# Two attentions of a fused transformer block: who copies and normalises the turned output, who scales the rows of maxima, and in which blocks the loads are issued

## The chip, the cores and the metric

The kernel runs on one core of one Trainium2 chip. The metric is the time of one execution in microseconds of the device, the median of three runs. A core has a matrix engine (TensorE, PE in the profile, with PEld for its weight loads), VectorE (DVE), ScalarE (ACT), GpSimd (POOL) and SyncE (SP), each with its own instruction queue; they meet in semaphores. DMAs are issued by POOL on queue q0 and by SP on queue q1, and are worked off by 16 DMA engines.

## The reference

```
x = x + L0(groupnorm(x))            # attention with relative positions, 12 heads of 16, 1024 tokens per image
t = tokens(x)
t = t + L1_attn(layernorm(t))       # attention without them
t = t + L1_ffn(layernorm(t))        # 16 experts, each token goes to one

L0:      attn = q*scale @ k^T + rel_h[..., :, None] + rel_w[..., None, :]
         out  = softmax(attn) @ v ;  return out @ proj_w + proj_b
L1_attn: softmax(q @ k^T / sqrt(192)) @ v
```

The batch is 8 images of 1024 tokens with 192 channels. The change is in `attention`, which computes the scores, the softmax and the product with v of both attentions.

## The kernel before

The stages follow one another: projections of the first attention (p1), the first attention (a1, with relative positions), output projection and projections of the second (p2), the second attention (a2), routing and experts. `attention` is called twice, with `rel` true and false.

One attention is 24 **steps**, one for each image and group of 4 heads. Steps come in pairs (u = 0, 1) with two sets of buffers; the first and the last pair are written out, the ten between them are a loop on each engine. A step has 16 **blocks**: 2 halves of the queries (512 each) times 8 tiles of 128 keys. In a block PE computes the 4 heads' scores, keys on partitions, into psS (L371); ACT takes the exponential into a_probs, two heads at a time (L458); PE multiplies by the values of the block before (L382, "pv"), which sums the turned output, 4 heads of 32 rows by 512 queries, in psO over the 8 key tiles. The value tile's 17th column is one, so that the row sums come along.

Exponentials need each query's row maximum beforehand. So PE also computes, one to two steps ahead, scores with queries on partitions from other buffers (a_qmax, a_kmax and, for even steps, h_qmax, h_kmax), 64 "max" jobs a step, 4 in a block (L353), and DVE reduces each to its maximum (L503). After the last of them, in block 12, DVE joins the two halves of the keys (L508). In block 13 a "rows" job turns the 128 by 32 maxima on PE (L357), DVE scales them to f16 (L513), and SP stores them as an extra row of a_qrows (L266), so that the score matmul subtracts them. From block 13 on (MAXBLK) the max jobs belong to the step after next; their buffers' loads are waited for at the start of that block (loadedm).

When a half is done, ACT copies the turned output out of psO (L449), a "back" job, four transposes on PE (L361), turns it back, DVE takes the reciprocal of the row sums (L520) and multiplies (L523), and SP stores the result (L280). Back jobs run at the end of blocks 2 (for the half before) and 10.

Max, rows and back jobs share psR, a ring of three PSUM banks: job n may start when job n-3 has been read. All readers of the ring are on DVE:

```
elif j[0] == "rows":                 # L513
    nc.vector.tensor_scalar(MT[:, :], psR[0:UNITS, slot, 0:P], -1.0 / MAXSCALE, None, ALU.mult)
else:                                # L520, L523
    nc.vector.reciprocal(RC[:, :, :], o[:, :, HD:HD + 1])
    nc.vector.tensor_tensor(OS[:, qh, :, :], o[:, :, 0:HD], RC..., ALU.mult)
```

The order on PE in a block is: scores of both pairs, two max jobs, pv of the block before, (rows in block 13,) two max jobs, (back in blocks 2 and 10).

Loads for later steps are issued by POOL, block by block. POOL's entry for block k waits until pv of block k-1 is done, which PE runs in the middle of its block k. `load_maxima` (L214) loads a_qmax and a_kmax, or the h_ ones, for the step after next: in a1 in entries 0 to 4, in a2 in entries 0 to 7, one query and one key part in each. `load` (L225) loads a_qrows, a_krows and a_v for the next step: the terms of queries and keys in a1 in entries 5, 6, 7 (three of 128 KB in each), rows for relative widths and heights in entries 8 to 11 (256 KB and 64 KB); in a2 the terms in entries 8 to 11; values in 12 and 13. In a1 SP also writes, two blocks ahead, 8 rows for relative heights into a_qrows before each block with kt >= 2 (`rel_rows`, L274, a_qrows<-relh, 32 KB); PE waits for them (relrow) at the start of that block.

Of the kernel before, what the change touches and what calls it, by code (L numbers as in the profile page):

```python
# [13 lines left out]
P = 128  # L14
# [4 lines left out]
GH = 4  # L19
# [23 lines left out]
def attention(nc, name, rel, scale, QK, RL, RLH, VN, OD, onehot_dram, head, early=None):  # L43
# [13 lines left out]
    with ExitStack() as ctx:  # L57
# [19 lines left out]
        OT = sb("outT", [P, QH, 512], F32)  # L77
        RC = sb("recip", [P, 4 * GH, 1], F32)
# [16 lines left out]
        ring_free = sem("ring_free")  # L95
        maxed = sem("maxed")
# [11 lines left out]
        SCORES, PVS, HALFS = 2 * BLK, BLK, QH  # L108

        def jobs_of(u, first, last):  # L110
            after = [[] for _ in range(BLK + 1)]
            for blk in range(BLK):
                offset, j = (1, EARLY + PER_BLK * blk) if blk < MAXBLK else (2, PER_BLK * (blk - MAXBLK))
                if not (last and u + offset >= 2):
                    after[blk] += [("max", j + i, offset) for i in range(PER_BLK)]
# [7 lines left out]
            return after  # L123

        FIRST = [("max", j, 0) for j in range(HALVES)] + [("rows",)] + [("max", j, 1) for j in range(EARLY)]
        PROLOGUE = len(FIRST)

        def number(first, last):
            at, out = 0, []
            for u in range(2):  # L130
                after = []
                for js in jobs_of(u, first, last):
                    after.append([(at + n, j) for n, j in enumerate(js)])
                    at += len(js)
                out.append(after)
            return out, at
# [4 lines left out]
        BASE0 = PROLOGUE  # L141
        BASE1 = PROLOGUE + N_FIRST

        def base_of(i):
            return BASE1 + (i - 1) * N_BODY
# [4 lines left out]
        def slot_free(n):  # L150
            return n + 2 if n < 2 else n + 1

        assert N_BODY % 3 == 2
        SHIFT = (1 - (BASE1 - 1)) % 3

# [3 lines left out]
        def back_number(jobs, u, which, qh):  # L159
            return next(n for js in jobs[u] for n, j in js if j[0] == "back" and j[1] == which and j[2] == qh)  # L160

        def rows_number(jobs, u):
            return next(n for n, j in jobs[u][MAXBLK] if j[0] == "rows")

        def max_of(j):
            r, half, p, qt = j % 2, j // 2 % 2, j // 4 % 2, j // 8
            return r, half, p, qt, r * 16 + p * 8 + qt
# [13 lines left out]
        def _(pool):  # L181
            def load_terms(s, buf, n):
                at = slice(HD * n, HD * n + HD)
                for c in range(NA):
                    pool.dma_start(A[buf][c][at, :, :], qk(s, TERMS[n][0], 0)).then_inc(loaded[buf], 16)  # L185
                pool.dma_start(K[buf][at, :, :], qk(s, TERMS[n][1], 1)).then_inc(loaded[buf], 16)

            def load_rel(s, buf, c, half):
                w, h = QR + WI * half, RH + 4 * half
                pool.dma_start(A[buf][c][w:w + WI, :, :], rel_w(s, half)).then_inc(loaded[buf], 16)  # L190
                if half == 0:
                    pool.dma_start(A[buf][c][RH:RH + 8, :, :], RLH[s, c].rearrange("i (k h) t -> (i k) h t", h=GH))\
                        .then_inc(loaded[buf], 16)
# [5 lines left out]
            def load_max_terms(s, buf, r, n):  # L199
                of = slice(64 * r + HD * n, 64 * r + HD * n + HD)  # L200
                pool.dma_start(AM[buf][0][of, :, :], qk_pair(s, TERMS[n][0], 0, r)).then_inc(loadedm[buf], 16)  # L201
                pool.dma_start(KM[buf][of, :, :], qk_pair(s, TERMS[n][1], 1, r)).then_inc(loadedm[buf], 16)

            def load_max_rel(s, buf, r, half):
                am, at = AM[buf][half], 64 * r
                if half == 1:
                    pool.dma_start(am[at:at + HD, :, :], qk_pair(s, 0, 0, r)).then_inc(loadedm[buf], 16)
                pool.dma_start(am[at + HD:at + HD + WI, :, :],
                               RL[s, 0].rearrange("(k r p) t -> r k p t", p=2, r=2)[r]).then_inc(loadedm[buf], 16)
                pool.dma_start(am[at + HD + WI:at + 64, :, :],  # L210
# [3 lines left out]
            def load_maxima(s, buf, blk):  # L214

                if rel:
                    if blk == 0:
                        load_max_terms(s, buf, 0, 0)
                        load_max_terms(s, buf, 1, 0)
                    elif blk < 5:  # L220
                        load_max_rel(s, buf, blk % 2, (blk - 1) // 2)
                elif blk < 8:
                    load_max_terms(s, buf, blk % 2, blk // 2)

            def load(s, buf, blk):  # L225

                if rel:
                    if blk in (5, 6, 7):
                        load_terms(s, buf, blk - 5)
                    elif blk in (8, 9, 10, 11):  # L230
                        load_rel(s, buf, blk % 2, (blk - 8) // 2)
                elif blk in (8, 9, 10, 11):
                    load_terms(s, buf, blk - 8)
                if blk in (12, 13):
                    load_values(s, buf, blk - 12)

# [3 lines left out]
            for blk in range(BLK):  # L240
# [4 lines left out]
            pool.wait_ge(ring_free, HALVES + 4)  # L245

            def step(s, u, last):
                for blk in range(BLK):
                    pool.wait_ge(pvdone, s * PVS + blk + 2)
                    nc.gpsimd.sem_inc(paced, 1)  # L250
                    if not last:
                        load_maxima(s + 2, u, blk)
                    load(s + 1, 1 - u, blk)

            with pool.Fori(0, ITERS - 1) as i:
                for u in range(2):
                    step(2 * i + u, u, False)
            step(STEPS - 2, 0, True)

        @block.sync  # L260
        def _(sp):
            def row_of_maxima(buf, free):

                sp.wait_ge(ring_free, free)
# [12 lines left out]
            def store(s, qh, base, n):  # L277

                sp.wait_ge(ring_free, base + n + 4)
# [27 lines left out]
            row_of_maxima(0, HALVES + 4)  # L307

            def step(i, u, jobs, base, first, last):
# [4 lines left out]
                for blk in range(BLK):  # L314
# [11 lines left out]
                    if blk == 4 and not (first and u == 0):  # L326
                        store(s - 1, 1, base, back_number(jobs, u, -1, 1))
                    if blk == KT + 4:
                        store(s, 0, base, back_number(jobs, u, 0, 0))
                if more:  # L330
                    row_of_maxima(1 - u, base + rows_number(jobs, u) + 4)
                else:
                    store(s, 1, base, back_number(jobs, u, 0, 1))
# [12 lines left out]
        def _(pe):  # L346
            def job(jn, j, base, slot, free, buf, halves, rows):
                pe.wait_ge(ring_free, base + free)
                if j[0] == "max":
                    r, half, p, qt, _ = max_of(j[1])  # L350
                    b = (buf + j[2]) % 2
                    at = slice(64 * r, 64 * r + MR)
                    mm = nc.tensor.matmul(psR[:, slot, :], AM[b][half][at, p, P * qt:P * qt + P],  # L353
                                          KM[b][at, p, 512 * half:512 * half + 512], start=True, stop=True)
# [10 lines left out]
            def scores_pair(buf, kt, qh, pair, n, pairs):  # L365

                pe.wait_ge(exped, pairs + n + 1)
                for j in range(2):
                    keys, queries = slice(P * kt, P * kt + P), slice(512 * qh, 512 * qh + 512)
# [16 lines left out]
            def step(i, u, jobs, base, first, last, slot, free):  # L386
# [1432 lines left out]
```

## Time and profile before

| what | value |
|---|---|
| median of 3 runs | 3230.5 us (3227.85 to 3234.65) |
| span of the profiled execution, first to last instruction | 3278.2 us, 47.7 us over that median; no time around it is given |
| busy: PE, DVE, ACT, POOL | 2922.2, 2439.8, 1849.7, 1061.6 us |
| mean granted TensorE clock | 0.906 |

The span is read by stages: scores of a1 start between 365 and 1457 us, those of a2 between 1796 and 2841 us. Within an attention the timeline (instructions in order of time, merged where they follow one another) repeats with the block. A row of the timeline gives the start, the length, the engine, the line of the kernel, the operation, output<-input, the number of instructions, and in brackets the engine's idle time before it and what ended it. "SPq" and "POOL ... DMA" rows are issues of DMAs, not transfers.

### The profile page before, as it was taken

To read this page: it belongs to the slowest core of one execution; us is meant where nothing else is said; L and a number is where in the kernel's file an instruction comes from. 1 tells how busy PE (TensorE), PEld (TensorE's weight loads), DVE (VectorE), ACT (ScalarE), POOL (GpSimd) and SP (SyncE) were. 2 spreads that over 40 slices of the span, in tenths; PEclk is the share of its full clock that TensorE was granted. 3 is DMA by queue.
4 is the path that set the end of the run, shared out by engine and by line. 5 is a ranking of instruction groups with operands and counts; after the bars stand their busy time and mean duration, and the time that the engine had idled before them with its cause. 6 is when DMAs were issued, how large, how long until landed. Compare 5 with 4: busy or idle time off the path is not lost. (4 is left out here: it accounts for less than half of the span.)

```text
span 3278.2 us, 63755 instructions
## 1 busy us (share of the span) xinstructions
PE 2922.2 (89%) x17818; PEld 1147.0 (35%) x17818; DVE 2439.8 (74%) x4430; ACT 1849.7 (56%) x2379; POOL 1061.6 (32%) x1714
## 2 busy tenths in 40 slices
PE   5886999999999999977897999999999999871887
PEld 4664122222222222215652222222222222361666
DVE  4544899999999999933547999999999999451221
ACT  2433376667776677663440677777777777610332
POOL 0012233333333333213232333232333332155665
PEclk9776799999999999998995999999999999965777
DMA  6776554555445554433654622222222222350211
GB/s 126 219 237 184 104 103 98 100 110 107 102 101 100 111 103 100 90 61 121 206 160 98 124 72 70 72 75 75 73 76 75 70 71 63 97 89 12 58 54 35
DMA packets 222364, 327.92 MB, mean 100 GB/s; under 512 B 63820, under 2 KB 150550, under 8 KB 217650
## 3 DMA queue, kind: packets, MB, share of 16 engines
q0 software_dynamic: 79488, 202.00, 27.3%
q1 hardware_dynamic: 142772, 124.60, 14.5%
q8 instruction: 56, 0.92, 0.1%
q14 instruction: 48, 0.39, 0.1%
HBM read 217.71 MB, written 109.19 MB: 100 GB/s over the span
## 5 line engine op out<-in xcount | busy, mean ns | idle before, releaser
L458 ACT ACTIVATE a_probs<-a_psS 128x1024 f32<-128x1024 f32 x1536 | 1488.5, 1021 | 738.5 <-PE a_psS L371 734.0
L503 DVE TENSOR_REDUCE h_halfmax<-a_psR 128x1 f32<-128x512 f32 x1536 | 979.7, 686 | 73.5 <-PE a_psR L353 64.3
L503 DVE TENSOR_REDUCE a_halfmax<-a_psR 128x1 f32<-128x512 f32 x1536 | 984.2, 686 | 63.6 <-PE a_psR L353 54.5
L371 PE MATMUL a_psS<-a_qrows,a_krows 121*128 121x512 f16 (+1 forms) x3072 | 804.2, 383 | 44.8 <-DMA a_qrows<-relh 40.2
L382 PE MATMUL a_psO<-a_probs,a_v 128*32 128x512 f32 x6144 | 824.0, 609 | 1.2 <-ACT a_probs L458 1.2
L353 PE MATMUL a_psR<-h_kmax,h_qmax 64*128 64x512 f16 x1536 | 357.9, 405 | 40.8 <-POOL h_ident L39 40.1
L371 PEld LDWEIGHTS a_psS<-a_qrows,a_krows 121*128 121x128 f16 (+1 forms) x3072 | 241.8, 98 | 417.7 <-issue 161.5
L353 PE MATMUL a_psR<-a_kmax,a_qmax 64*128 64x512 f16 x1536 | 325.6, 393 | 1.8 <-DVE a_halfmax L503 1.4
L353 PEld LDWEIGHTS a_psR<-h_kmax,h_qmax 64*128 64x128 f16 x1536 | 81.9, 93 | 539.1 <-DVE h_halfmax L503 471.6
L353 PEld LDWEIGHTS a_psR<-a_kmax,a_qmax 64*128 64x128 f16 x1536 | 78.9, 93 | 490.4 <-DVE a_halfmax L503 460.1
L185 POOL DMA_DIRECT2D a_qrows<-qk x240 | 124.1, 517 | 264.5 <-PE a_psO L382 262.0
L861 PE MATMUL p_psQ<-p_xnT,p_wqk 96*128 96x512 f32 x384 | 183.0, 640 | 16.0 <-DVE p_xnT L1015 13.9
L382 PEld LDWEIGHTS a_psO<-a_probs,a_v 128*32 128x32 f32 x6144 | 121.2, 108 | 183.3 <-issue 176.3
L201 POOL DMA_DIRECT2D h_qmax<-qk x110 | 56.3, 512 | 358.4 <-PE a_psO L382 305.2
L1628 DVE TENSOR_TENSOR e_y<-e_psY,e_x 128x192 f32<-128x192 f32 x80 | 28.6, 357 | 191.1 <-PE e_psY L1553 106.6
L201 POOL DMA_DIRECT2D a_qmax<-qk x120 | 61.4, 512 | 301.3 <-PE a_psO L382 300.5
L1049 DVE SCALAR_TENSOR_TENSOR p_half<-p_qk,p_sc,p_half 128x2048 f16<-128x2048 f32 (+1 forms) x36 | 71.5, 1997 | 103.1 <-ACT p_half L958 103.1
L951 ACT ACTIVATE p_qk<-p_psQ,p_bqk 128x512 f32<-128x512 f32 x96 | 65.9, 686 | 114.6 <-PE p_psQ L861 114.6
L1590 ACT COPY e_xmT<-e_psX 96x256 f32<-96x256 f32 x80 | 29.5, 369 | 175.0 <-PE e_psX L1547 130.5
L861 PEld LDWEIGHTS p_psQ<-p_xnT,p_wqk 96*128 96x128 f32 x384 | 77.5, 206 | 117.1 <-issue 107.3
L190 POOL DMA_DIRECT2D a_qrows<-rel x96 | 48.6, 506 | 205.6 <-PE a_psO L382 205.6
L197 POOL DMA_DIRECT2D a_v<-v x96 | 53.8, 560 | 185.4 <-PE a_psO L382 184.7
(185 smaller groups left out, 2755.2 us busy)
## 6 DMA issues: line engine op xcount, KB each, us to landing
a_qrows<-qk POOLq DMA_DIRECT2D x240, 128.0 KB, 4.2
qk<-p_half SPq DMA_DIRECT2D x96, 256.0 KB, 3.3
a_qrows<-rel POOLq DMA_DIRECT2D x96, 256.0 KB, 4.2
a_v<-v POOLq DMA_DIRECT2D x96, 256.0 KB, 3.1
a_krows<-qk POOLq DMA_DIRECT2D x168, 128.0 KB, 4.5
v<-p_v SPq DMA_DIRECT2D x36, 512.0 KB, 5.7
relh<-p_rel SPq DMA_DIRECT2D x48, 256.0 KB
attn<-a_out SPq DMA_DIRECT2D x96, 128.0 KB, 2.3
```

The costliest lines, as they stand in the source:

```text
L185: pool.dma_start(A[buf][c][at, :, :], qk(s, TERMS[n][0], 0)).then_inc(loaded[buf], 16)
L190: pool.dma_start(A[buf][c][w:w + WI, :, :], rel_w(s, half)).then_inc(loaded[buf], 16)
L197: pool.dma_start(V[buf][:, x, :, :], VN[s][:, x, :, :]).then_inc(loaded[buf], 16)
L201: pool.dma_start(AM[buf][0][of, :, :], qk_pair(s, TERMS[n][0], 0, r)).then_inc(loadedm[buf], 16)
L353: mm = nc.tensor.matmul(psR[:, slot, :], AM[b][half][at, p, P * qt:P * qt + P], KM[b][at, p, 512 * half:512 * half + 512], start=True, sto ...
L371: mm = nc.tensor.matmul(psS[:, (2 * n + j) % 4, :], K[buf][:, h, keys], A[buf][kt % NA][:, h, queries], start=True, stop=True)
L382: mm = nc.tensor.matmul(psO[32 * h:32 * h + 32, :], V[buf][:, kt, h, :], PT[:, blk % 2, h, :], start=(kt == 0), stop=(kt == KT - 1))
L458: nc.scalar.activation(PT[:, blk % 2, 2 * pair:2 * pair + 2, :], psS[:, b0:b0 + 2, :], ACT.Exp, scale=scale).then_inc(exped, 1)
L503: nc.vector.tensor_reduce(mx[:, unit, half:half + 1], psR[:, slot, :], AX.X, ALU.max)\
L861: mm = nc.tensor.matmul(psQ[:, n % 2, :], WQK[:, c, P * m:P * m + P], XN[:, c, 512 * q:512 * q + 512], start=(c == 0), stop=(c == 1))
L951: nc.scalar.activation(QF[:, m, 512 * q:512 * q + 512], psQ[:, n % 2, :], ACT.Identity, bias=BQK[:, m:m + 1], scale=1.0).then_inc(qf, 1)
L1049: half = nc.vector.scalar_tensor_tensor(HL[1][:, m, tokens], QF[:, m, tokens], SC[:, m:m + 1], HL[0][:, m, tokens], ALU.mult, ALU.subtract)
```

## The change

The psR ring gets two more readers. ACT copies the turned output of a back job from psR to a new SBUF tile a_outTurned (semaphore copied); DVE takes the reciprocals from there; POOL multiplies, in its entries 4 and 12, ahead of that entry's loads (semaphore normed); SP's store waits for normed. ACT also scales the rows of maxima. ACT does both between the exponentials of two blocks, DVE the reciprocal a block later, after that block's first two reductions. Ring slots freed by ACT are counted apart from those that DVE frees. The rows job moves behind the last two max jobs of block 13; in the first 64 maxima before step 0 it moves behind two jobs of the next step.

```diff
-                after[MAXBLK].insert(2, ("rows",))
+                after[MAXBLK].append(("rows",))
...
+            def normalise(steps, qh):
+                pool.wait_ge(recips, steps * QH + qh + 1)
+                pool.wait_ge(stored[qh], steps * 16 + 16)
+                nc.gpsimd.tensor_tensor(OS[:, qh, :, :], OB[:, :, 0:HD], RC[:, :, :].to_broadcast([P, 4 * GH, HD]),
+                                        ALU.mult).then_inc(normed, 1)
...
+                if j[0] == "rows":
+                    nc.scalar.activation(MT[:, :], psR[0:UNITS, slot, 0:P], ACT.Copy, scale=-1.0 / MAXSCALE).then_inc(copied, 1)
+                else:
+                    half = s * QH + j[1] * QH + j[2]
+                    act.wait_ge(normed, half)
+                    nc.scalar.copy(OB[:, :, :].rearrange("p x v -> p (x v)"), psR[:, slot, :]).then_inc(copied, 1)
...
+            def reciprocals(at, base, s):
+                dve.wait_ge(copied, base[2] + at[2] + 1)
+                dve.wait_ge(normed, half)
+                nc.vector.reciprocal(RC[:, :, :], OB[:, :, HD:HD + 1]).then_inc(recips, 1)
```

The loads are the same ones, issued in other entries:

```diff
             def load_maxima(s, buf, blk):
+                if rel and 2 <= blk < 6:
+                    load_max_query(s, buf, blk % 2, (blk - 2) // 2, 0)
+                    load_max_height(s, buf, blk % 2, (blk - 2) // 2)
+                elif rel and blk in (6, 7):
+                    load_max_key(s, buf, blk % 2, 0)
+                elif rel and 8 <= blk < 12:
+                    load_max_width(s, buf, blk % 2, (blk - 8) // 2)
+                if not rel and blk < 8:
+                    load_max_query(s, buf, blk % 2, 0, blk // 2)
+                elif not rel and 8 <= blk < 12:
+                    load_max_key(s, buf, 0, blk - 8)
+                    load_max_key(s, buf, 1, blk - 8)
             def load(s, buf, blk):
                 if rel:
+                    if blk < 3:
+                        load_query(s, buf, 0, blk)
+                        load_query(s, buf, 1, blk)
+                    elif blk < 7:
+                        load_width(s, buf, blk % 2, (blk - 3) // 2)
+                    elif blk == 7:
+                        load_key(s, buf, 0)
+                        load_key(s, buf, 1)
+                    elif blk == 8:
+                        load_key(s, buf, 2)
+                        load_height(s, buf, 0)
+                        load_height(s, buf, 1)
                 elif blk < 8:
+                    (load_query(s, buf, 0, blk // 2) if blk % 2 == 0 else load_key(s, buf, blk // 2))
```

PE's waits for these loads (loaded at block 0, loadedm at block 13, relrow) stand where they stood.

First place: POOL in the loop of a1, first step of a pair, entries 6 to 9 (a1_qrows1, a1_krows1: the next step's buffers; h1_qmax0: those of the maxima two steps on). Before:

```order
L185 DMA a1_qrows1_0<-qk1 16x4x1024
L185 DMA a1_qrows1_1<-qk1 16x4x1024
L186 ISA
L186 DMA a1_krows1<-qk1 16x4x1024
L249 REGISTER_ALU
L190 DMA a1_qrows1_0<-rel1 32x4096
L192 DMA a1_qrows1_0<-relh1 8x4096
L249 REGISTER_ALU
L190 DMA a1_qrows1_1<-rel1 32x4096
L192 ISA
L192 DMA a1_qrows1_1<-relh1 8x4096
```

and now, entries 7 to 9:

```order
L224 DMA h1_kmax0<-qk1 16x2x1024
L204 ISA
L204 DMA a1_krows1<-qk1 16x4x1024
L204 ISA
L204 DMA a1_krows1<-qk1 16x4x1024
L291 REGISTER_ALU
L228 DMA h1_qmax0_0<-rel1 32x2048
L204 DMA a1_krows1<-qk1 16x4x1024
L211 DMA a1_qrows1_0<-relh1 8x4096
L211 ISA
L211 DMA a1_qrows1_1<-relh1 8x4096
```

The run of nine query and key loads followed by the width and height rows is gone; query terms and widths went to entries 0 to 6, and one width part for the maxima is now issued in each of entries 8 to 11.

Second place: POOL in the loop of a2, entries 10 to 13. Before:

```order
L185 DMA a2_qrows1<-qk2 16x4x1024
L186 DMA a2_krows1<-qk2 16x4x1024
L249 REGISTER_ALU
L197 ISA
L197 DMA a2_v1<-v2 128x512
```

and now:

```order
L224 DMA h2_kmax0<-qk2 16x2x1024 x2
L291 REGISTER_ALU
L224 DMA h2_kmax0<-qk2 16x2x1024 x2
L291 REGISTER_ALU
L274 ISA
L275 REGISTER_ALU
L276 TENSOR_TENSOR a2_out<-a2_outTurned,a2_recip 128x256
L216 ISA
L216 DMA a2_v1<-v2 128x512
```

The key parts for the maxima two steps on moved here, two in each of entries 8 to 11, and the multiplication stands ahead of the first values.

Third place: PE in the loop of a2, block 13 from its pv on (psR is the ring). Before:

```order
L382 MATMUL a_psO<-a_probs,a_v 32x512 x4
L348 REGISTER_ALU
L356 REGISTER_ALU
L357 MATMUL a_psR<-h_ident,h_rowmax 32x128
L348 REGISTER_ALU
L353 MATMUL a_psR<-h_kmax,h_qmax 128x512
```

and now:

```order
L435 MATMUL a_psO<-a_probs,a_v 32x512 x4
L401 REGISTER_ALU
L406 MATMUL a_psR<-h_kmax,h_qmax 128x512
L401 REGISTER_ALU
L406 MATMUL a_psR<-h_kmax,h_qmax 128x512
L401 REGISTER_ALU
L409 REGISTER_ALU
L410 MATMUL a_psR<-h_ident,h_rowmax 32x128
```

The turning of the maxima moved behind the pair of max jobs.

## Rows read from the trace of the kernel before

**Rows 1.** The page: its first row.
```profile
span 3278.2 us, 63755 instructions
```
**Rows 2.** Line L371 (scores): a1's stretch, then a2's; starts of first and last.
```profile
L371 PE MATMUL a_psS<-a_qrows,a_krows x1536: 377/379/634, 365.0 to 1456.5; 121*128 121x512 f16 x192
...
L371 PE MATMUL a_psS<-a_qrows,a_krows x1536: 377/379/634, 1796.4 to 2840.4; 65*128 65x512 f16 x192
```
**Rows 3.** Timeline of a2, one block: scores, two maxima, pv, next scores.
```profile
2162.76 1.04 PE L371 MATMUL a_psS<-a_qrows,a_krows 65*128 65x512 f16 x4
...
2163.74 0.39 PE L353 MATMUL a_psR<-a_kmax,a_qmax 64*128 64x512 f16 x2
...
2164.05 1.06 PE L382 MATMUL a_psO<-a_probs,a_v 128*32 128x512 f32 x8
...
2165.38 1.04 PE L371 MATMUL a_psS<-a_qrows,a_krows 65*128 65x512 f16 x4
```
**Rows 4.** Busy time by engine, 82 us inside a2: PE, PEld, DVE, ACT, POOL.
```profile
2132.00:2214.00 82.00, 81.63 (x498) 21.96 (x496) 79.35 (x132) 59.79 (x64) 25.57 (x50) 1.00 0.29 76
```
**Rows 5.** Timeline before step 0 of a2: DVE's 64 reductions, then scaling the rows.
```profile
1750.65 38.36 DVE L503 TENSOR_REDUCE h_halfmax<-a_psR 128x1 f32<-128x512 f32 x64 [15.70 <-PE a_psR L353]
...
1789.80 0.28 DVE L513 TENSOR_SCALAR h_rowmaxT<-a_psR 32x128 f16<-32x128 f32 x1 [0.56 <-PE a_psR L357]
```
**Rows 6.** What PE waited for in a1, 400 to 1440 us: total, times, longest.
```profile
PE a_psS L371 <- DMA a_qrows<-relh: 37.9, 22, 2.4
```
**Rows 7.** Timeline of a1, blocks 8 to 10: issue of rows, scores.
```profile
805.03 7.50 SPq L274 DMA_DIRECT2D a_qrows<-relh  x3
...
806.43 1.04 PE L371 MATMUL a_psS<-a_qrows,a_krows 121*128 121x512 f16 x4
...
810.66 1.03 PE L371 MATMUL a_psS<-a_qrows,a_krows 121*128 121x512 f16 x4 [1.55 <-DMA a_qrows<-relh]
```
**Rows 8.** DMA issues, 799 to 811 us: KB each, median us to landing.
```profile
a_qrows<-qk POOLq DMA_DIRECT2D x6, 128.0 KB, 4.5
```
**Rows 9.** DMA issues, 785 to 799 us, the same.
```profile
a_qmax<-rel POOLq DMA_DIRECT2D x4, 128.0 KB, 2.6
a_qmax<-qk POOLq DMA_DIRECT2D x4, 64.0 KB, 2.3
```
**Rows 10.** Timeline of a1: POOL's entry 11, then PE's scores of block 13.
```profile
817.22 0.49 POOL L190 DMA_DIRECT2D a_qrows<-rel  x1 [3.03 <-PE a_psO L382]
...
819.41 1.04 PE L371 MATMUL a_psS<-a_qrows,a_krows 121*128 121x512 f16 x4
```
**Rows 11.** Timeline of a2: POOL's entry 11, then PE's scores of block 13.
```profile
2184.71 0.51 POOL L185 DMA_DIRECT2D a_qrows<-qk  x1 [2.10 <-PE a_psO L382]
...
2185.25 0.51 POOL L186 DMA_DIRECT2D a_krows<-qk  x1
...
2186.86 1.04 PE L371 MATMUL a_psS<-a_qrows,a_krows 65*128 65x512 f16 x4
```
**Rows 12.** Timeline of a2, block 13 from pv to the next scores.
```profile
2188.15 1.06 PE L382 MATMUL a_psO<-a_probs,a_v 128*32 128x512 f32 x8
...
2189.15 0.28 PE L357 MATMUL a_psR<-h_ident,h_rowmax 128*32 128x128 f32 x1
...
2189.37 0.76 PE L353 MATMUL a_psR<-h_kmax,h_qmax 64*128 64x512 f16 x2
...
2190.06 1.04 PE L371 MATMUL a_psS<-a_qrows,a_krows 65*128 65x512 f16 x4
```
**Rows 13.** Timeline of a2 after a back job: ACT, DVE.
```profile
2160.88 1.94 ACT L458 ACTIVATE a_probs<-a_psS 128x1024 f32<-128x1024 f32 x2 [1.28 <-PE a_psS L371]
...
2161.35 0.43 DVE L523 TENSOR_TENSOR a_out<-a_psR,a_recip 128x256 f32<-128x256 f32 x1
```
**Rows 14.** Groups by line: ACT's copy of psO, and POOL's addition of a bias.
```profile
L449 ACT COPY a_outT<-a_psO 128x512 f32<-128x512 f32 x96 | 56.7, 591 | 5.5 <-PE a_psO L382 3.6
...
L791 POOL TENSOR_TENSOR p_x<-p_x,p_bproj 128x3072 f32<-128x3072 f32 x4 | 26.7, 6686 | 32.6 <-DMA p_x<-in_x 32.6
```

More of the change, by code:

```diff
@@ L107, in attention, with max_of @@
         NREL = 6
-        SCORES, PVS, HALFS = 2 * BLK, BLK, QH
+        SCORES, PVS = 2 * BLK, BLK
+        def max_of(j):
+            r, half, p, qt = j % 2, j // 2 % 2, j // 4 % 2, j // 8
+            return r, half, p, qt, r * 16 + p * 8 + qt
         def jobs_of(u, first, last):
-            after = [[] for _ in range(BLK + 1)]
+            before, after = [[] for _ in range(BLK + 1)], [[] for _ in range(BLK + 1)]
             for blk in range(BLK):
@@ L140, in attention, with other_number @@
         JOBS_LAST, _ = number(False, True)
-        BASE0 = PROLOGUE
-        BASE1 = PROLOGUE + N_FIRST
+        BASE1 = tuple(x + y for x, y in zip(BASE0, N_FIRST))
+        assert N_BODY[0] % 3 == 2
         def base_of(i):
-            return BASE1 + (i - 1) * N_BODY
+            return tuple(x + (i - 1) * y for x, y in zip(BASE1, N_BODY))
         def slot_of(n):
             return n % 3
[L150 to L154, printed above, removed]
+        SHIFT = (1 - (BASE1[0] - 1)) % 3
         def first_slot(m):
             return (m + SHIFT) % 3
[L159 to L167, printed above, removed]
+        def other_number(jobs, u, job):
+            return next(at[2] for a, b in jobs[u] for at in a + b if at[3] == job)
         block = ctx.enter_context(nc.Block())
@@ L403, in last_pv @@
[L403 to L407 removed]
                     scores_pair(u, kt, qh, 0, 2 * blk, 2 * blks)
                     scores_pair(u, kt, qh, 1, 2 * blk + 1, 2 * blks)
[L411 to L413 removed]
+                    for at in before:
+                        job(at, base, slot(at[0]), u, halves, s + 1)
@@ new lines, in step @@
+            def step(i, u, jobs, base, first, last, slot):
+                s = 2 * i + u
+                for blk in range(BLK):
+                    for at in jobs[u][blk - 1][1] if blk > 0 else []:
+                        if at[3][0] != "max":
+                            other(at, base, slot(at[0]), s)
+                    for pair in range(2):
+                        n = 2 * blk + pair
+                        act.wait_ge(scores, s * SCORES + n + 1)
+                        act.wait_ge(pvdone, s * PVS + blk + 1)
+                        b0 = 2 * n % 4
+                        nc.scalar.activation(PT[:, blk % 2, 2 * pair:2 * pair + 2, :], psS[:, b0:b0 + 2, :], ACT.Exp,
+                                             scale=scale).then_inc(exped, 1)
+                    if blk == 0 and not (first and u == 0):
+                        copy_out(s - 1, 1)
+                    if blk == KT:
+                        copy_out(s, 0)
+                if last and u == 1:
+                    copy_out(s, 1)
+                    for at in jobs[u][BLK][1]:
+                        other(at, base, slot(at[0]), s)
@@ L481, in _ @@
+            for at in FIRST:
+                if at[3][0] == "rows":
+                    other(at, (0, 0, 0), first_slot(at[0]), None)
             for u in range(2):
-                step(0, u, True, False, before_first)
-            step_1 = before_in(base_of(1), BASE0, JOBS_FIRST, JOBS)
+                step(0, u, JOBS_FIRST, BASE0, True, False, lambda n: first_slot(BASE0[0] + n))
+            with act.Fori(1, ITERS - 1) as i:
+                for u in range(2):
+                    step(i, u, JOBS, base_of(i), False, False, slot_of)
```

292 lines of the change are left out of this document (137 added, 155 removed).

## Prediction

> **What bounds the kernel now.** I read the span first [rows 1], then the two stages that the change touches. Both attentions issue the same 1536 score matmuls; from first to last a1 takes 1456.5 - 365.0 = 1091.5 us, a2 2840.4 - 1796.4 = 1044.0 us [rows 2]. So a1 loses 47.5 us that a2 doesn't.
>
> Then one block in the timeline. From scores to scores it takes 2165.38 - 2162.76 = 2.62 us, and the pieces touch: the maxima start 0.98 us after the scores, pv 0.31 us after them, the next scores 1.33 us after pv with two more maxima between [rows 3]. No piece waits: PE is busy for 81.63 of 82 us. DVE is busy for 79.35 of them and looks like a bound too [rows 4]. It isn't quite. Where nothing else paces DVE, before step 0, it does 64 reductions in 38.36 us, 0.60 each [rows 5]; four make 2.40 us, 0.2 us less than a block. PE sets the pace, DVE follows closely behind.
>
> Last, what stops PE in a1: the rows for relative heights, 22 times in the steady part, 37.9 us in all, up to 2.4 us at once [rows 6]. One case: SP issues the rows for block 10 at 805.03, block 9 starts at 806.43, and block 10 should start 2.62 us later, at 809.05, but starts at 810.66 [rows 7]. So the rows took some 5.5 us. In that stretch the 128 KB query loads, three per block with the key, take a median of 4.5 us [rows 8]; in the calmer stretch before it a 128 KB load takes 2.6 us and a 64 KB load 2.3 us [rows 9]. The rows are late because nine loads of 128 KB are issued ahead of them in three blocks, faster than they land.
>
> **The change part by part.** The sum is made against the profiled execution, whose span of 3278.2 us [rows 1] lies 47.7 us above the median of the runs; I take the differences over to the median unscaled.
>
> *Multiplication and row scaling leave DVE.* Per step that is 2 x 0.43 us [rows 13] and 0.28 us [rows 5], 1.14 us; the reciprocals stay. Worth nothing on the path, since PE paces the block; if DVE were the cover that is gone, see the first rival.
>
> *ACT's copies.* The copy of the turned output has the size of the copy out of psO, 0.59 us [rows 14]. It falls in the gap after a back job, where ACT sat idle for 1.28 us waiting for the next scores [rows 13]. What queues behind it, the next exponentials, then starts at most 0.1 us later, and pv needs these only a block later. Row scaling is smaller and falls in the same kind of gap. Cost: zero, at most 3 x 0.1 us a step.
>
> *POOL's multiplication.* 3072 elements per partition took 6.69 us [rows 14], 2.2 ns each, so 256 take 0.56 us; with a start-up of as much again 1.1 us. Before that entry's loads: entry 12's values are needed in the next step, three blocks later. Cost zero. SP's store now waits for it, and the height rows of blocks 7 and 15 queue behind the store; they have two blocks, so I take zero here too and count any lateness in the fourth term.
>
> *The loads* are the same in number, and carry the sum.
>
> 1. The nine loads no longer pile up ahead of the heights: -47.5 us. The waits counted directly give 37.9 [rows 6], the lower bound; I take the difference of the stages, since their other work is equal.
>
> 2. In a1 one width part of 128 KB now leaves in entry 11, and PE waits for it before the scores of block 13, not only before the maxima. Entry 11 issues at 817.22, block 13 starts at 819.41: 2.19 us [rows 10]. At 2.6 us for landing [rows 9] PE stands for 0.41 us in each of the 22 steps that load maxima: +9.0 us. Bounds: 0, and 4.5 - 2.19 = 2.3 us a step if it lands as in the crowded stretch [rows 8]. I take the calm row, since entries 9 to 11 issue one load each.
>
> 3. In a2 entry 11 issues two key parts, the second 0.54 us after the first, as the two loads there do now, with 2186.86 - 2184.71 = 2.15 us to block 13 [rows 11]. A 64 KB load takes 2.3 us [rows 9]: 0.54 + 2.3 - 2.15 = 0.69 us, 22 times: +15.2 us. Bounds: 0.5 and, crowded, 2.9 us a step. The Trainium skill (DMA: Bandwidth & Descriptors, Anatomy of one DMA) gives a DMA a fixed 2.0 us and its bytes at 436 GB/s; by it, as an estimate, the key would land after 2.15 us and the sum would be 3 us less, but it would also have the 128 KB loads land in 2.3 us, where the trace shows 4.5.
>
> 4. Height rows that are still late: entries 2 to 5, 7 and 8 issue three or four loads. Between 0 and 0.9 us a step; block 12, behind entry 8's key and two height parts, is the likeliest. I take 0.4 us: +8.8 us.
>
> 5. The turning of the maxima. Today pv to the next scores takes 1.91 us in block 13 [rows 12] against 1.33 in another block [rows 3], 0.58 more: 0.22 us for the transposition, the rest because the last maxima no longer run as a pair. Behind the pair, the transposition costs between 0.22 and 0.58 us. And a PE that stood at the start of block 13 finds DVE further ahead. I take a gain of 0.2 us in the 44 steps that wait: -8.8 us.
>
> 6. The ends. The two early maxima ahead of the turning cover DVE's wait and scaling of 0.56 + 0.28 us [rows 5] before each step 0; the last half of each attention passes through ACT, DVE and POOL, about 1 us longer than now. Zero, bounds -2 and +2 us.
>
> Sum: -47.5 + 9.0 + 15.2 + 8.8 - 8.8 = -23.3 us. The span would be 3254.9, the median **3207 us**.
>
> **The rivals.**
>
> *DVE is the bound after all.* For it: 97% busy [rows 4]. The Trainium skill (Perfetto Trace Analysis, Optimizing Scalar/DVE Operations) says that moving work to ScalarE or GpSimd may make sense where DVE is saturated. Against it: 0.60 us a reduction [rows 5] and a PE without gaps. It would give 48 x 1.14 = 55 us more: 3152 us. Chance 0.05.
>
> *The height rows stay late, elsewhere.* The change would not spread evenly enough: four loads in entry 2, 7 and 8 still outrun the DMAs, and half of the 47.5 us stays; likewise if profiling itself stretches these waits, as 47.7 us between span and median allow. 3207 + 24 = 3231 us. Chance 0.15.
>
> *The last loads land late: slower.* Its place is the start of block 13. The backlog of entry 8, with two height parts, reaches the widths behind it, and these land as in the crowded stretch: 2.3 us a step, 50.6 us in a1 [rows 8, 10], in place of terms 2 and 4. Sum: -47.5 + 50.6 + 15.2 - 8.8 = +9.5, 3240 us. It decides from an average of (47.5 + 8.8 + 6.5) / 44 = 1.4 us of new waits a step; my terms hold 0.75. For it: every one of these loads was moved to its latest entry. Against it: one load an entry behind the backlog. Chance 0.10.
>
> *The heights aren't held up by the loads at all.* Then their waits stay whole, and with terms 2, 3 and 5 the time is 3230.5 + 15.4 = 3246 us. Against it: the rows land when the load issued just ahead of them does, at some 5.5 us [rows 7, 8]. The Trainium skill (DMA: Bandwidth & Descriptors, Queues, rings and completion order) has each DMA engine take turns between queues packet by packet, by which SP's rows would pass POOL's loads; the trace doesn't agree. Chance 0.05.
>
> **How the numbers follow.** My forecast has 0.65; its own range is 3188 (terms 2, 3 and 4 at 0, 0.5 and 0.2 us a step, term 5 at -10 us) to 3222 (term 1 at its lower bound of 37.9 us, term 4 at 0.65 us a step). The range that leaves out no more than 2 in 10 reaches from 3184 to the third rival, 3240. A measurement of this kernel tells 0.2%, 6.5 us, from no change. Faster by more: 0.63 of the forecast's 0.65, 0.05 of the first rival and 0.03 of the second's 0.15, 0.71. Within: the rest of both, 0.14. Slower: the last two, 0.15.
>
> **What would show it.** Right: in a1 the scores' wait for the height rows falls from 37.9 us to under 10; a wait for loads at block 13 of about 0.4 us in a1 and 0.7 in a2 appears; the block stays at 2.62 us; DVE is less busy at the same pace; a2's scores take longer than 1044.0 us by 5 to 15. Wrong: a block shorter than 2.6 us (DVE was the bound), a2 no longer than now (terms 3 and 5), or height waits above 20 us (term 1).

## The result and the profile after

The changed kernel takes 3271.2 us (median of 4 runs, 3262.0 to 3279.5) against 3229.8 for the kernel before on the same chip: a ratio of 1.0124, 95% interval 1.0102 to 1.0146. It is 41 us slower. The prediction was 3207, with a range to 3240: it had the sign wrong.

The page of the changed kernel begins with its span, which answers to [rows 1]:

```profile
span 3277.8 us, 63934 instructions
```

That is as long as the span of before [rows 1], though the medians differ by 41 us. So the first profile of before can't serve for the difference, and one experiment (before_again, below) took a second one. Here are the busy times by stage, of that second profile of before and then of the changed kernel. The stages end at the first and last scores of each attention and at the experts' first gather: projections, a1, the middle, a2, routing, experts. The columns are the stretch, its length, busy time (and instructions) of PE, PEld, DVE, ACT and POOL, granted clock, DMA share and GB/s.

```profile
0.00:365.70 365.70, 284.94 (x2846) 187.81 (x2847) 199.79 (x411) 114.36 (x254) 48.60 (x89) 0.74 0.70 184
365.70:1458.60 1092.90, 1045.64 (x6261) 275.58 (x6261) 971.69 (x1602) 765.29 (x813) 364.21 (x695) 0.99 0.48 99
1458.60:1796.70 338.10, 271.00 (x1065) 161.57 (x1061) 166.61 (x396) 102.58 (x192) 98.82 (x103) 0.80 0.51 145
1796.70:2840.00 1043.30, 1037.28 (x6260) 275.17 (x6259) 969.98 (x1603) 765.25 (x813) 297.77 (x580) 0.99 0.30 75
2840.00:3005.20 165.20, 77.21 (x438) 68.79 (x434) 71.30 (x261) 21.68 (x68) 85.86 (x87) 0.61 0.40 72
3005.20:3230.70 225.50, 173.05 (x960) 136.96 (x960) 56.92 (x160) 78.27 (x241) 163.02 (x160) 0.95 0.21 57
```

```profile
0.00:369.20 369.20, 285.54 (x2845) 187.69 (x2845) 199.49 (x410) 114.63 (x255) 47.62 (x87) 0.74 0.69 182
369.20:1454.10 1084.90, 1038.56 (x6261) 274.22 (x6261) 947.45 (x1533) 795.92 (x883) 396.13 (x744) 0.99 0.43 100
1454.10:1794.20 340.10, 266.18 (x1065) 160.66 (x1061) 171.76 (x394) 103.41 (x194) 99.52 (x104) 0.82 0.50 144
1794.20:2873.80 1079.60, 1046.55 (x6260) 276.23 (x6259) 949.47 (x1533) 794.70 (x883) 327.65 (x627) 0.98 0.26 73
2873.80:3050.60 176.80, 81.26 (x438) 72.26 (x434) 70.72 (x260) 22.69 (x69) 86.40 (x88) 0.59 0.35 68
3050.60:3277.80 227.20, 171.94 (x960) 133.66 (x960) 56.52 (x160) 78.10 (x241) 163.06 (x160) 0.96 0.20 57
```

Line by line: a1 got only 8.0 us shorter and a2 36.3 us longer (against [rows 2], counted as there to the very last matmul, 6.0 and 36.3); the middle got 2.0 us longer, routing 11.6, the projections 3.5 and the experts 1.7. VectorE is 20 to 24 us less busy in each attention, as the change intends, and no block became shorter by it.

**a2: one queue stands still.** What PE waited for in the steady part (what, us in total, times, longest): first a1, 400 to 1440 us, in before_again (this answers to [rows 6]), then the same in the changed kernel, then its a2, 1830 to 2840 us:

```profile
PE a_psS L371 <- DMA a_qrows<-relh: 39.5, 23, 2.4
...
PE a_psS L424 <- DMA a_qrows<-relh: 26.9, 33, 2.2
PE a_psS L424 <- DMA h_qmax<-rel: 4.6, 11, 0.6
PE a_psS L424 <- DMA a_qmax<-rel: 4.3, 11, 0.5
...
PE a_psS L424 <- DMA a_kmax<-qk: 18.0, 11, 3.3
PE a_psS L424 <- DMA h_kmax<-qk: 7.6, 11, 0.8
```

In a2 the waits for `h_kmax` (even steps) are alike, 0.7 us each. Those for `a_kmax` (odd steps) aren't: 18.0 us in 11 waits, up to 3.3 us. The timeline of step 8 and then of step 7, the key parts of entry 11 and the scores of block 13:

```profile
2191.59 1.04 POOL L224 DMA_DIRECT2D h_kmax<-qk  x2 [2.18 <-PE a_psO L435]
2194.54 0.82 PE L424 MATMUL a_psS<-a_qrows,a_krows 65*128 65x512 f16 x3 [0.72 <-DMA h_kmax<-qk]
...
2145.54 1.05 POOL L224 DMA_DIRECT2D a_kmax<-qk  x2 [4.72 <-PE a_psO L435]
2148.47 1.08 PE L424 MATMUL a_psS<-a_qrows,a_krows 65*128 65x512 f16 x4 [3.23 <-DMA a_kmax<-qk]
```

In step 7 GpSimd was idle 4.72 us ahead of its loads, 2.5 more than in step 8. This comes back in steps 11, 15 and 19, always at this entry: every 104 loads. PE stands for 3.23 us, and its granted clock then falls to the lower level. Three stretches of step 11, the wait and the two blocks behind it (PEclk is the third value from the end):

```profile
2324.30:2330.20 5.90, 2.76 (x18) 0.66 (x16) 4.75 (x9) 2.07 (x3) 2.17 (x4) 1.00 0.10 29
2330.20:2335.20 5.00, 4.92 (x17) 0.97 (x18) 1.34 (x3) 1.94 (x2) 0.00 (x0) 0.50 0.22 71
2335.20:2340.00 4.80, 4.80 (x17) 0.87 (x15) 2.52 (x4) 2.21 (x3) 0.55 (x1) 0.50 0.46 131
```

So the two blocks after the wait take 5.0 and 4.8 us at a clock of 0.50. The four steps last 50.0 us on average (48.3 to 51.2), the others 44.5, and 43.8 in before. The loss of a2 is 18 x 0.7 and 4 x 6.2 us, 37.4, near the 36.3 of the stage. Of the 25 us of the four steps some 13 are the waits themselves, the rest the slow blocks behind them.

GpSimd stood like that in before too. In step 7 of a2 in its first profile, at an entry with five blocks in hand:

```profile
2127.00 0.51 POOL L201 DMA_DIRECT2D a_qmax<-qk  x1 [1.50 <-PE a_psO L382]
...
2131.78 0.51 POOL L201 DMA_DIRECT2D a_qmax<-qk  x1 [3.73 <-PE a_psO L382]
```

That is 2.2 us more idle time than one block earlier. Nobody waited for it there.

**a1: the rows are late elsewhere.** In two steps of a1 the scores of block 4, then of block 5 (step 14), and of blocks 5 and 6 (step 15):

```profile
1023.42 1.04 PE L424 MATMUL a_psS<-a_qrows,a_krows 121*128 121x512 f16 x4
1026.82 1.03 PE L424 MATMUL a_psS<-a_qrows,a_krows 121*128 121x512 f16 x4 [0.72 <-DMA a_qrows<-relh]
...
1071.13 1.04 PE L424 MATMUL a_psS<-a_qrows,a_krows 121*128 121x512 f16 x4
1076.04 1.03 PE L424 MATMUL a_psS<-a_qrows,a_krows 121*128 121x512 f16 x4 [2.23 <-DMA a_qrows<-relh]
```

The lateness left block 10 [rows 7] and came to blocks 5, 6, 7 and 11. SP isn't the reason: in every step of every kernel here it issues each of these rows within 0.2 us of the end of the scores that it waits for, so the rows are late on their way. Step 15 is one of those in which GpSimd stands, in a1 every third step (93 loads), at entry 2: these six steps last 47.1 us on average, the others 45.2.

**The ends.** From the last turning (PE) to GpSimd's first instruction of routing, in before_again and then in the changed kernel; then, of the changed kernel, the line of the block's end (durations in ns, least, median, most):

```profile
2844.52 0.63 PE L361 MATMUL a_psR<-h_ident,a_outT 128*128 128x128 f32 x4 [0.80 <-ACT a_outT L449]
2845.93 0.33 SPq L280 DMA_DIRECT2D attn<-a_out  x1
2848.10 0.20 POOL L37 MEMSET r_ident<- 128x128 f32 x1 [43.49 <-POOLq L57]
```

```profile
2878.33 0.63 PE L414 MATMUL a_psR<-h_ident,a_outT 128*128 128x128 f32 x4 [0.80 <-ACT a_outT L495]
2879.94 0.62 POOL L276 TENSOR_TENSOR a_out<-a_outTurned,a_recip 128x256 f32<-128x256 f32 x1 [9.31 <-DVE a_recip L562]
2880.59 0.33 SPq L331 DMA_DIRECT2D attn<-a_out  x1
2888.24 0.21 POOL L37 MEMSET r_ident<- 128x128 f32 x1 [7.68 <-POOLq L57]
...
L57 POOLq DRAIN  x2: 7357/7724/8091, 1460.2 to 2879.9; - x2
```

It took 3.6 us, and takes 9.9; at the end of a1 it took 3.6 and takes 9.2. At the block's end GpSimd drains its queue, for 7.4 and 8.1 us. Before, it had nothing to do in the last step and drained beside it. Now the drain comes after the last multiplication, and the next stage waits for it: 5.6 + 6.3 = 11.9 us. The two stages grew by 13.6 us together, but by 2.0 and 11.6, so each of them also holds some 4 or 5 us of other differences, which no run here explains.

### The profile page after: what moved, and what is told of

Its sections match the earlier page's. It is cut to its first block and busy times, and to the rows that moved or that the text cites. A ratio compares the mean times of both kernels' runs of the same rounds, so it can differ in the third digit from the quotient of the medians.

```text
span 3277.8 us, 63934 instructions
## 1 busy us (share of the span) xinstructions
PE 2890.0 (88%) x17818; PEld 1104.7 (34%) x17818; DVE 2395.4 (73%) x4286; ACT 1909.4 (58%) x2523; POOL 1120.4 (34%) x1810
## 5 line engine op out<-in xcount | busy, mean ns | idle before, releaser
L406 PE MATMUL a_psR<-h_kmax,h_qmax 64*128 64x512 f16 x1536 | 352.5, 405 | 45.2 <-POOL h_ident L39 44.5
L220 POOL DMA_DIRECT2D h_qmax<-qk x132 | 68.4, 518 | 268.4 <-PE a_psO L435 241.2
L220 POOL DMA_DIRECT2D a_qmax<-qk x144 | 74.5, 518 | 224.6 <-PE a_psO L435 219.2
L1669 DVE TENSOR_SCALAR e_xm<-e_x 128x192 f32<-128x192 f32 x80 | 30.8, 385 | 144.5 <-DMA e_x<-x,e_slots 143.6
L276 POOL TENSOR_TENSOR a_out<-a_outTurned,a_recip 128x256 f32<-128x256 f32 x96 | 59.1, 615 | 200.1 <-PE a_psO L435 180.4
L952 PE MATMUL p_psR<-p_half,p_relThalf 64*128 64x64 f16 x1920 | 98.2, 240 | 15.0 <-DVE p_rel L1134 12.5
```

What stands on the lines that cost most here:

```text
L220: pool.dma_start(AM[buf][half][of, :, :], qk_pair(s, TERMS[n][0], 0, r)).then_inc(loadedm[buf], 16)
L276: nc.gpsimd.tensor_tensor(OS[:, qh, :, :], OB[:, :, 0:HD], RC[:, :, :].to_broadcast([P, 4 * GH, HD]), ALU.mult).then_inc(normed, 1)
L406: mm = nc.tensor.matmul(psR[:, slot, :], AM[b][half][of, p, P * qt:P * qt + P], KM[b][of, p, 512 * half:512 * half + 512], start=True, sto ...
L952: mm = nc.tensor.matmul(o[:, :, x, :], table.rearrange("p k h -> p (k h)"), q[:, :, xx, :] if hw == 0 else q[:, :, :, xx], start=(i == 0), ...
```

## The experiments

Stages are taken from first to last scores, as above. The runs come from several chips; each ratio is to the kernel before on the same chip, so a difference between two kernels is best read from the ratios.

| kernel | median, us | ratio to before, 95% | a1 | a2 | PE waits for height rows, a1 |
|---|---|---|---|---|---|
| before_again | 3232.4 (one) | | 1092.9 | 1043.3 | 39.5 |
| the changed kernel | 3271.2 | 1.0124 [1.0102, 1.0146] | 1084.9 | 1079.6 | 26.9 |
| a2_loads_back | 3226.0 | 0.9982 [0.9971, 0.9992] | 1085.1 | 1038.2 | 28.3 |
| moves_only | 3250.7 | 1.0053 [1.0034, 1.0072] | 1105.4 | 1040.8 | 46.4 |
| loads_only | 3258.0 | 1.0082 [1.0063, 1.0102] | 1083.4 | 1079.5 | 27.5 |
| wait_behind_scores | 3235.9 | 1.0018 [1.0007, 1.0029] | 1075.0 | 1055.9 | 25.6 |
| end_on_vector | 3258.3 | 1.0068 [1.0045, 1.0090] | 1080.4 | 1076.8 | 26.5 |
| keys_one_earlier | 3230.6 | 1.0003 [0.9990, 1.0016] | 1086.0 | 1038.3 | 26.5 |
| three_mended | 3206.6 | 0.9918 [0.9901, 0.9935] | 1069.4 | 1037.9 | 23.3 |
| four_mended | 3198.9 | 0.9892 [0.9875, 0.9909] | 1060.1 | 1040.8 | 15.2 |
| five_mended | 3215.5 | 0.9953 [0.9936, 0.9969] | 1073.8 | 1038.4 | 30.8 |
| heights_last | 3190.2 | 0.9883 [0.9858, 0.9907] | 1056.0 | 1040.8 | 7.0 |

**before_again.** No edit.

> The kernel before, unchanged, for a second look at its stages. Theory one: the 48 us between the first profiled execution and the timed runs lay in the last stage, which ran at a lower granted clock (262 us from the first gather to the end, where the other kernels' profiles show 222 to 227). Then this one shows a span of 3225 to 3245 us, a1 at 1085 to 1100, a2 at 1041 to 1046 us. Theory two: the profile itself stretches a1's waits for height rows; then the span is 3270 to 3280 us again.

Theory one holds: 3230.7 us, a1 1092.9, a2 1043.3, experts 225.5. The first profile's 48 us lay in the experts (36 us) and routing (11 us). So my doubt whether profiling stretches a1's waits is settled: it doesn't.

**a2_loads_back.** Change to the diff: in a2 the loads go where they were.

```diff
-                elif not rel and 8 <= blk < 12:
-                    load_max_key(s, buf, 0, blk - 8)
-                    load_max_key(s, buf, 1, blk - 8)
+                    load_max_key(s, buf, blk % 2, blk // 2)
...
-                elif blk < 8:
-                    (load_query(s, buf, 0, blk // 2) if blk % 2 == 0 else load_key(s, buf, blk // 2))
+                elif 8 <= blk < 12:
+                    load_query(s, buf, 0, blk - 8)
+                    load_key(s, buf, blk - 8)
```

> The changed kernel, with a2's bulk loads back in their old order: max queries and max keys in entries 0 to 7, the terms in entries 8 to 11. Theory one, the last loads: a2 got 36 us longer because the last max keys now leave GpSimd in entry 11 and block 13 waits for them, 0.8 us in most steps and over 3 us in four of them, where GpSimd itself stands for 2.5 us at that entry. Then no such wait is left, a2's scores last 1040 to 1046 us and the time is 3235 us, plus or minus 6. Theory two, the moved work: ScalarE's copy and GpSimd's multiplication hold something up in a2. Then a2 stays at 1070 to 1080 us and the time at 3265 to 3275.

a2 fell by 41.4 us to 1038.2, and the time by 45: theory one. The moved work holds up nothing in a2.

**moves_only.** The loads of a1 are put back as well, to the order of the kernel before.

> Only the work that moved between engines (copy on ScalarE, multiplication on GpSimd, scaling on ScalarE, the turning of the maxima behind the pair); the loads of both attentions as before. Theory one, the last loads: the moves cost nothing, a2 lasts 1040 to 1046 us, a1 1085 to 1095 us with its waits for height rows back at 30 to 40 us in blocks 10 and 11, and the time is within 8 us of the kernel before, 3230. Theory two, the moved work: a2 at 1070 us or more, the time at 3260 or more.

a2 is as theory one has it, but the time isn't: 0.5% above before. Two costs were missing. The ends are longer here too (middle 342.4, routing 171.3 us, together 10 us more than in before_again), and a1 takes 12.5 us more, with its waits for rows at 46.4 us. In a1 the half output is now stored two blocks later, beside the query loads, and a 128 KB key load takes a median of 5.8 us to land instead of 5.4. That the store is the cause was not tried alone, so the cause of these 12.5 us stays open.

**loads_only.** The kernel before with the load functions of the change and their order; nothing else.

> Only the new order of the bulk loads; copy, multiplication and scaling stay on VectorE as before. Theory one, the last loads: a2 is as long as in the changed kernel, 1070 to 1085 us, with about 25 us of waits for max keys at block 13, and the time is 3260 to 3275 us. Theory two, the moved work: a2 lasts 1050 us at most, and the time is 3235 us or less.

As theory one: a2 1079.5 us, 25.1 us of waits for max keys, the same four long steps. It is 13 us faster than the whole change, about the cost of the ends. Loads alone (0.8% slower) and moves alone (0.5%) add up to about the change (1.2%).

**wait_behind_scores.**

```diff
-                    if blk == MAXBLK and not last:
-                        pe.wait_ge(loadedm[u], i * (16 * NLOADM) + 32 * NLOADM)
...
                     scores_pair(u, kt, qh, 1, 2 * blk + 1, 2 * blks)
+                    if blk == MAXBLK and not last:
+                        pe.wait_ge(loadedm[u], i * (16 * NLOADM) + 32 * NLOADM)
```

> The changed kernel, with PE's wait for the max loads moved from ahead of block 13's scores to behind them, where the first maxima need the loads. Theory one, the last loads: the scores last 1.03 us, so the steady waits of 0.8 us (a2) and 0.5 us (a1) vanish, and in the four steps in which GpSimd stands about 2.2 us are left; a2 lasts 1050 to 1065 us, a1 about 8 us less than now, the time is 3235 to 3255 us. Theory two, the moved work: block 13 stays as slow, a2 at 1070 us or more, and the time at 3262 or more.

As theory one: a2 lasts 1055.9 us, a1 9.9 us less, and the steady waits are gone. Of PE's waits for loads in a2 one kind is left, in the four steps, 1 us shorter each:

```profile
PE a_psR L406 <- DMA a_kmax<-qk: 9.1, 4, 2.3
```

The clock fell to 0.50 behind two of these four waits, in steps 11 and 15; step 11 still lasts 51.3 us, step 7 only 46.1.

**end_on_vector.**

```diff
-            normalise(STEPS - 1, 1)
...
                 for at in jobs[u][BLK][1]:
                     reciprocals(at, base, 2 * i + u)
+                    dve.wait_ge(recips, STEPS * QH)
+                    dve.wait_ge(stored[1], STEPS * 16)
+                    nc.vector.tensor_tensor(OS[:, 1, :, :], OB[:, :, 0:HD], RC[:, :, :].to_broadcast([P, 4 * GH, HD]),
+                                            ALU.mult).then_inc(normed, 1)
```

> The changed kernel, with the very last multiplication of each attention on VectorE instead of GpSimd, so that GpSimd's closing drain (7.4 and 8.1 us in the changed kernel, behind that multiplication) runs beside the last blocks, as it did before. Theory one, the drain: from the turned output to the next stage's first instruction it takes 3 to 4 us instead of 8.6 and 9.3 us, twice some 5.5 us, and the time is 3256 to 3263 us. Theory two, the ends cost nothing but their own instructions: the time stays within 4 us of the changed kernel's 3271.

3258.3, 13 us less, and by the ratios 18: the time is as theory one has it. The two ends, counted from the start of the last turning, take 4.6 and 5.3 us instead of 9.2 and 9.9 (counted from its end, 4.0 and 4.7, so the second is above the forecast), and 9.2 us come from there. a1 and a2 are also 4.5 and 2.8 us shorter in this profile, for which the edit gives no reason.

**keys_one_earlier.** The keys in `7 <= blk < 11`, with `blk - 7`.

> The changed kernel, with a2's max keys in entries 7 to 10 instead of 8 to 11, nothing else. Theory one, the last loads: one entry is 2.6 us, so the 0.8 us that block 13 waits in most steps vanish; where GpSimd stands, it is at another place or at most one wait of 0.9 us is left in such a step; a2 lasts 1037 to 1046 us, 33 to 40 us less than the changed kernel, and the time is 3230 to 3240 us. Theory two: two key parts in one entry, with the query order around them, are slow wherever they stand; then a2 stays at 1060 us or more, the time at 3255 or more.

a2 1038.3 us: theory one. GpSimd still stands for 2.5 us in steps 7, 11, 15 and 19, now at entry 10, and a block in hand covers it. So 41 us of a2 hung on one entry.

**three_mended.** a2_loads_back, wait_behind_scores and end_on_vector together.

> The changed kernel with three things mended: a2's loads in their old order, PE's wait for the max loads behind block 13's scores, the last multiplication on VectorE. Theory one (each is a cause of its own): a2 at 1036 to 1041 us, a1 at 1070 to 1080 us, the two ends some 11 us shorter; 3226 - 10 - 11 = 3205 us, plus or minus 6, ratio to the kernel before 0.990 to 0.994. Theory two (they overlap): 3215 us or more.

3206.6: the causes add up, and this kernel beats both.

**four_mended.** In a1 entries 0 to 2 bring two query parts each, 3 the first max queries and heights, 4 and 5 a width part each, 6 two width parts and the max keys, 7 a key and max queries, 8 a max width and the heights of blocks 0 and 1, 9 and 10 the other max widths and heights, 11 two keys.

> As three_mended, and a1's loads spread anew: 256 KB in each entry, no more than two to four loads, except entry 6, behind which no height row is on its way (640 KB), the max loads by entry 10 and the last keys in entry 11. Theory one: height rows are late where the entries issued around them bring more than 256 KB, so a1's waits for them fall from about 27 us to below 10 in the steady part, a1 lasts 1050 to 1060 us, and the time is 3185 to 3195 us. Theory two: the rows are late by GpSimd's standing at entry 2 and by chance landings, whatever the spread; then a1 stays at 1068 us or more and the time within 5 us of three_mended.

Between the two theories: rows wait 15.2 us, a1 lasts 1060.1. The lateness of blocks 5 to 7 is mostly gone, though GpSimd stands every third step as before; blocks 10 and 11 still wait. The new spread changes bytes, kinds and places of the loads at once, so it doesn't show which of them counts.

**five_mended.** The two height loads of entry 8 change places with the two max keys of entry 6.

> As four_mended, with the two height loads of entry 8 in entry 6 and the two max keys of entry 6 in entry 8. Theory one: blocks 10 and 11 still wait in four_mended because the height loads, into 8 partitions each, land slowly between the rows of blocks 10 and 11; in entry 6 no row is on its way, so the waits fall from 15 us to below 10, a1 to 1053 to 1057 us, and the time to 3191 to 3197 us. Theory two: it is the bytes of an entry that count, which stay the same; then a1 stays within 3 us of 1060 and the time within 3 us of 3199.

Worse, against both theories: rows wait 30.8 us, mostly in block 10, whose row is issued 1.8 us behind the second height load of entry 6 (and 3.4 us behind the first load of that entry). I had held that entry to be free of rows, and it isn't. From step 1 to 21 block 10 now waits 24.6 us instead of 3.0, and block 11, behind entry 8, no longer waits, instead of 7.4: the lateness went with the height loads, which changed places with loads of the same 64 KB.

**heights_last.** The height loads in entry 13 with a key, the values in 11 and 12, the other keys in 7 and 8.

> As four_mended, with a1's two height loads in entry 13, behind which no row is issued for another 6 us, one key beside them, and the values one entry earlier; 256 KB an entry as before, entry 6 as in four_mended. Theory one: it is the two height loads, into 8 partitions each, that hold up the rows issued behind them (in five_mended even 3.4 us behind them, where block 10 waited 1.2 us); then the waits for rows fall from 15 us to 8 or less, a1 lasts 1047 to 1054 us, and the time is 3186 to 3193 us, ratio 0.985 to 0.988. Theory two: any 256 KB around a row make it late now and then; then a1 stays at 1057 to 1064 us and the time at 3196 to 3202.

```profile
PE a_psS L428 <- DMA a_krows<-qk: 8.2, 7, 1.5
PE a_psS L428 <- DMA a_qrows<-relh: 7.0, 9, 1.7
```

The waits for rows fell to 7.0 us, and the time is where theory one has it, though a1 is 2 us above: the key in entry 13 is now late for the next step, 8.2 us. This is the fastest kernel, 3190.2 us. That the height loads hold up rows more than other loads do fits both runs. heights_last moved keys and values too; the exchange in five_mended is the cleaner test, but it was made in one place only. The 3.4 us in this run's expectation is the distance to the first load of entry 6, not to the height loads.

**terms_halved.** three_mended with each 128 KB load of a2 as two.

> three_mended, with each of a2's eight loads of 128 KB for the scores cut into two of 64 KB (by heads, so that each row of 2 KB stays whole): 34 loads a step instead of 26, the same bytes. It asks what GpSimd's standing of 2.3 us, once in 94 and 88 loads by turns in a2, goes by. By the number of loads: it comes after 2.7 steps on average instead of 3.5. By the bytes or rows: after 3.5 steps as before, in the same steps (7, 10, 14, 17, 21). The time is within 10 us of three_mended's 3207 either way.

GpSimd stood after 2.5 steps instead of 3.5, twice in every 170 loads. So it doesn't go by bytes; the number of loads is nearer, but not the whole of it, since the same 26 loads a step gave 94 and 88 by turns in the old order of a2 and 104 in the new one. (The time of its one run, 3226.2, is 20 us above three_mended's, outside what I expected; most of it lies in a1, 1081.7 us, which the edit doesn't touch.) One case, where GpSimd's last wait was already over (the multiplication ran) and it stood all the same:

```profile
2020.50 0.61 POOL L285 TENSOR_TENSOR a_out<-a_outTurned,a_recip 128x256 f32<-128x256 f32 x1 [1.15 <-PE a_psO L443]
2023.21 0.54 POOL L228 DMA_DIRECT2D a_qmax<-qk  x1 [2.09 <-issue]
```

## Why the prediction was wrong

The forecast was -23.3 us; between the two profiles (before_again and the changed kernel) it was +47.1, between the medians +41. The terms below come to +41; the projections and the experts, where nothing was changed, add 5.2.

| term | predicted, us | measured, us |
|---|---|---|
| 1 and 4: waits for height rows, a1 | -47.5 + 8.8 | -12.6 |
| 2: widths at block 13, a1 | +9.0 | +8.9 |
| 3: keys at block 13, a2 | +15.2 | +25.6 of waits; +37 with the low clock |
| 5: turning behind the pair | -8.8 | some -4 |
| 6: the ends | 0, within 2 | +11.9 |

- **Terms 1 and 4 failed, by 26 us.** "The nine loads no longer pile up ahead of the heights: -47.5" took the removal of one pile for the removal of the waits. The change made others: entries 2 to 5 bring 384 KB each around the rows of blocks 5 to 7, and entry 8 four loads ahead of block 11's. I had put the leftover at 0.4 us a step; it is 1.2. Which of bytes, number and kind made the rows late there wasn't separated. The second rival (half of the wait stays, elsewhere) is what happened in a1, with two thirds staying; its price of 3231 us fell short, since it left out what happened in a2 and at the ends. four_mended and heights_last show that another order does remove the waits. The Trainium skill (DMA: Bandwidth & Descriptors, Queues, rings and completion order) has each DMA engine take turns between queues packet by packet, from which I had concluded that SP's rows would pass GpSimd's loads. The waits went from 23.3 us (three_mended) to 7.0 (heights_last) and to 30.8 (five_mended) by moving GpSimd's loads alone, so the rows depend on them; whether the engines take turns, no run here shows.
- **Term 2 was right,** 0.4 us a step.
- **Term 3 was right in 18 steps and failed in four, by 22 us in all.** Predicted was 0.69 us; measured is 0.7 where GpSimd comes on time. What failed is "22 times": in steps 7, 11, 15 and 19 GpSimd stands for 2.5 us at just that entry. I took the two issue times of one step [rows 11] for those of all, and a row of before with 3.73 us of idle time in place of 1.5 lay in the same queue. Those four steps cost 25 us, some 12 of it in the slow blocks at the low clock. keys_one_earlier shows it: one entry earlier, with GpSimd standing as before, the whole of it is gone.
- **Term 5** had the right sign and was put at twice its size: in steps without waits block 13 takes 3.06 us instead of 3.19, and the next block 0.03 more, so the gain is 0.1 us a step (a2_loads_back).
- **Term 6 failed, by 12 us.** "About 1 us longer" counted the instructions, and not what GpSimd does behind its last one. end_on_vector gives 9.2 us of it back.
- **The moves cost nothing inside a2's blocks, as predicted** (a2_loads_back): a block still takes 2.61 us with less work on VectorE, so VectorE was not the bound, and the first rival falls. The multiplication takes 0.62 us, near the 0.56 without a start-up. The moves aren't free as a whole: moves_only is 0.5% slower than before, by the ends and by 12.5 us in a1 with the old loads, for which the prediction had no term.
- **The rival with the right sign** (last loads land late) named the place, block 13, and the wrong way to it: a1's widths of entry 11 landed as fast as forecast (a median of 2.55 us for 2.6), and the new waits average (8.9 + 25.6) / 44 = 0.8 us, below its 1.4. Its price also missed that the clock can fall behind a long wait.
- The 47.7 us between span and median lay in the last two stages, so taking the differences over unscaled did no harm. The 3.5 us of the projections aren't the change's: other kernels with its a1 loads start a1 between 362.0 and 367.4.

## What to carry to other kernels

A load moved to the last entry that still just makes it has its price set by the worst issue of that queue, not by a typical one: list the idle time ahead of every issue, over all steps, and leave one entry in hand. An engine that gets the last instruction of a stage brings its closing work onto the path; see what it does after that instruction now. And where one pile of transfers is cleared, work out what the new entries bring, and which loads it is, as carefully as for the old.

## What was not expected of the hardware

- GpSimd's queue stands for 2.1 to 2.5 us once in 84 to 104 loads, in every kernel here, at the same places in both profiles of the kernel before, more by the number of loads than by bytes. What it does then is open.
- Its drain at the end of an attention takes 5.1 to 8.1 us (9.9 in terms_halved); those of PE, ACT and DVE 0.3 to 0.7. Behind the last multiplication of a2 it takes 8.1 us with the new order of a2's loads and 5.8 with the old one (a2_loads_back, moves_only). The 2.3 us between are as long as one standing of the queue; that they are one is not shown.
- Each wait of PE of 3.2 us in the changed kernel's a2, a stage that otherwise has a clock of 1.00, was followed by blocks at 0.50, which is 1.2 of its 2.4 GHz, for 9.8 us in step 11; the waits of 0.7 us were not. Of the four waits of 2.3 us in wait_behind_scores two were followed by it.
